# Routing of tokens to experts: GpSimd in place of VectorE makes the low halves of the token rows

## The chip, the cores and the metric

The kernel runs on one core of one Trainium2 chip. The metric is device time in microseconds. Three runs of the kernel before took 1812.97, 1812.97 and 1817.88 us, median 1812.97. Engines are called as in the profile: PE (TensorE), DVE (VectorE), ACT (ScalarE), POOL (GpSimd), SP (SyncE, which issues DMAs here).

## The reference

Four residual blocks follow each other on `x` of 4 x 1024 tokens with 256 features: cross-attention, a mixture of experts, cross-attention, a mixture of experts. The change lies in what comes ahead of both mixtures. Cut to that:

```python
x = x + _L0_xattn_ref(ctx_768, _layernorm(x), ...)
x = x + _L0_ffn_ref(_layernorm(x), router_w, w1, b1, w2, b2)   # 8 experts, 2 per token
x = x + _L1_xattn_ref(_layernorm(x), ctx_768, ...)
x = x + _L1_ffn_ref(_layernorm(x), gate_w, w1, w2, w3)         # 8 experts, 2 per token

# in both mixtures, z = layernorm(x):
logits = z @ router                # (tokens, 8)
probs = softmax(logits)
top_w, top_idx = top_k(probs, 2)
top_w = top_w / (sum(top_w) + 1e-9)
out = sum over the two chosen experts of top_w * expert(z)
```

## The kernel before

The 4096 tokens are 32 tiles of 128 rows (`T` = 32, `TB` = 8 tiles to a batch, `B` = 4 batches). They stay in SBUF in `g.x` (`x_sb` in the profile). The kernel is a chain of stages, each with one instruction stream per engine: attention, `route`, `experts`, attention, `route`, `experts`. `route` (line 816 on) is run once for each layer; the profile names its tiles with the prefix `e_`.

`route` normalises each tile to `z`, a ring of `R` = 4 buffers in f32, and does two things with it. PE transposes it (L898), ACT copies the transpose out (L938) and PE multiplies it with the router for the logits (L907). And the row is stored for the experts as two f16 halves, high and low, which together hold the f32 value: ACT writes the high half as a cast of `z` (L943, `token_high`), and DVE writes the low half as `z` minus the high half (L989, `token_low`). Both halves take the place of the tile of `x` in SBUF (`parts` is `g.x` seen as f16). SP stores a batch of them to memory once its 8 low halves are done, and then issues two loads of expert weights (`bring_home`).

DVE's stream sets the order of this first part. It centers tiles 0 to 3 (`center`, L984). Then it goes through t = 0 to 31: the low half of tile t, which waits for the high half of t; then `center(t + 4)`, which waits until the low half of t is done, since it takes over the same buffer of the ring. Some tiles have more behind them. At t = 1 stand the statistics of the last batch (`summarise`, L312 to L322), for which POOL makes the reciprocal roots (L328). At t = 2 DVE waits until POOL has made its constants (`p_step`, L882 to L889). At t = 10, 18 and 26 `choose` runs for the batch before: it copies the logits of 8 tiles (L1004) and finds the two best experts in a chain of small steps, each of which waits for the one ahead (L1006 to L1021). At t = 13, 21 and 29 `weigh` makes the shares. The fourth `choose` comes behind the loop.

ACT goes through the tiles with a copy and a high half each. At t = 12, 20 and 28 it makes the exponentials of the batch before (L949, L950), for which it waits for the last step of `choose`.

In the second part of `route` DVE, ACT and PE turn the choices into lists of slots for the experts (L1054 to L1108). They need all four choices. The first indirect DMA of `experts` (L1197) gathers token rows by these lists.

POOL in `route` had only the roots, one memset, one affine select and six iotas.

Of the kernel before, what the change touches and what calls it, by code (L numbers as in the profile page):

```python
# [21 lines left out]
ALU = mybir.AluOpType  # L22
# [3 lines left out]
P = 128  # L26
B = 4
S = 1024
T = B * S // P
TB = S // P  # L30
D = 256
# [12 lines left out]
E = 8  # L44
# [259 lines left out]
def summarise(dve, g, run, t0, t1, twice):  # L304

    seen = 7 * (run - 1)
    tmp, ve = g.stat_tmp[:, :, t0:t1], g.stat_ve[:, t0:t1]
    stats, steps = g.stats[:, t0:t1, :], g.stat_steps  # L310

    dve.tensor_tensor(tmp[:, 0, :], stats[:, :, 1], stats[:, :, 4], ALU.add).then_inc(steps, 1)  # L312
    dve.tensor_tensor(tmp[:, 1, :], stats[:, :, 1], stats[:, :, 4], ALU.subtract).then_inc(steps, 1)
    dve.tensor_tensor(tmp[:, 2, :], stats[:, :, 2], stats[:, :, 5], ALU.add).then_inc(steps, 1)
    dve.wait_ge(steps, seen + 3)
    dve.tensor_scalar(g.mean[:, t0:t1], tmp[:, 0, :], 0.5, None, ALU.mult).then_inc(steps, 1)
    dve.tensor_tensor(tmp[:, 3, :], tmp[:, 1, :], tmp[:, 1, :], ALU.mult).then_inc(steps, 1)
    dve.wait_ge(steps, seen + 5)
    dve.scalar_tensor_tensor(tmp[:, 0, :], tmp[:, 3, :], D / 4, tmp[:, 2, :], ALU.mult, ALU.add).then_inc(steps, 1)
    dve.wait_ge(steps, seen + 6)  # L320
    grow, eps = (1.0 + LN_EPS, LN_EPS ** 2) if twice else (1.0, LN_EPS)
    dve.tensor_scalar(ve, tmp[:, 0, :], grow / D, eps, ALU.mult, ALU.add).then_inc(steps, 1)  # L322


def roots(pool, g, run, t0, t1):

    pool.wait_ge(g.stat_steps, 7 * run)
    pool.tensor_tensor(g.rstd[:, t0:t1], g.stat_ve[:, t0:t1], g.neghalf[:, t0:t1], ALU.pow).then_inc(g.stat_roots, 1)  # L328
# [455 lines left out]
C = 2  # L784
NT = (2 * B * S + E * (C * P - 1)) // (C * P)
# [7 lines left out]
LAST = (B - 1) * TB  # L793
# [13 lines left out]
def route(nc, g, layer):  # L807
# [7 lines left out]
    R = 4  # L815
# [3 lines left out]
    with ExitStack() as st:  # L819
        m = Mem(nc, st)  # L820
        nm = g.name
        z = m.sb(nm("z"), [P, R, D])
        parts = g.x[:].bitcast(F16)
# [5 lines left out]
        upper = m.sb(nm("upper"), [P, P])  # L829
        rev = m.sb(nm("rev"), [P, E])  # L830
        tiles = m.sb(nm("tiles"), [P, NT, E])
        ecol = m.sb(nm("ecol"), [P, NT])
        lanes = m.sb(nm("lanes"), [P, P])
        blocks = m.sb(nm("blocks"), [P, NT * C])
        spare = m.sb(nm("spare"), [P, NT * C])
        ids = m.sb(nm("ids"), [P, 2, T])
# [6 lines left out]
        cnt, cumt, base = (m.sb(nm(f"e{i}"), [P, E]) for i in range(3))  # L843
        passed = m.sb(nm("passed"), [P, T + 1, E])
# [8 lines left out]
        z_done, hi_done, lo_done = m.sem(nm("z_")), m.sem(nm("hi")), m.sem(nm("lo"))  # L853
        chosen, shifted, lanes_known = (m.sem(nm(n)) for n in ("chosen", "shifted", "lanes_known"))
        scanned = m.sem(nm("scanned"))
        t_done, ev, lg_done, p_step = m.sem(nm("t")), m.sem(nm("ev")), m.sem(nm("lg")), m.sem(nm("p"))
# [7 lines left out]
        @block.sync  # L864
        def _(sp):
            def store(b):
                sp.wait_ge(lo_done, TB * (b + 1))
                sp.dma_start(g.zrows[b * S:(b + 1) * S, :].rearrange("(t p) d -> p t d", p=P),
                             parts[:, b * TB:(b + 1) * TB, :]).then_inc(stored, 16)

            bring_home(sp, g, layer, 0)
            for b in range(B):
                store(b)
                if 1 + b < AHEAD:
                    bring_home(sp, g, layer, 1 + b)
            sp.wait_ge(stored, 16 * B)
            sp.wait_ge(g.x_home, 16 * B * (layer + 1))

        @block.gpsimd
        def _(pool):  # L880
            roots(pool, g, 3 + 2 * layer, LAST, T)
            pool.memset(passed[:, 0, :], 0.0).then_inc(p_step, 1)  # L882
            pool.affine_select(out=upper[:], in_=g.ones[:], compare_op=ALU.is_gt, fill=0.0, base=0,
                               pattern=[[1, P]], channel_multiplier=-1).then_inc(p_step, 1)
            for out, pattern, start, by_row in (
                    (rev[:], [[-1, E]], E, 0), (tiles[:], [[1, NT], [0, E]], 0, 0), (lanes[:], [[1, P]], 0, 0),
                    (blocks[:], [[P, NT * C]], 0, 0), (spare[:], [[0, NT], [P, C]], B * S, 1),
                    (ids[:], [[0, 2], [P, T]], -B * S, 1)):
                pool.iota(out, pattern=pattern, base=start, channel_multiplier=by_row,  # L889
                          allow_small_or_imprecise_dtypes=True).then_inc(p_step, 1)  # L890
        @block.tensor
        def _(pe):
            def turn(t):
# [86 lines left out]
        def _(dve):  # L980
            def center(t):
                if t >= R:
                    dve.wait_ge(t_done, t - R + 1)
                dve.tensor_scalar(z[:, t % R, :], g.x[:, t, :], g.mean[:, t:t + 1], g.rstd[:, t:t + 1],  # L984
                                  ALU.subtract, ALU.mult).then_inc(z_done, 1)

            def token_low(t):
                dve.wait_ge(hi_done, t + 1)
                dve.tensor_tensor(parts[:, t, D:2 * D], z[:, t % R, :], parts[:, t, 0:D], ALU.subtract  # L989
                                  ).then_inc(lo_done, 1)  # L990

            n = [0]

            def step(ins):
# [5 lines left out]
            def choose(b):  # L1000

                ts = slice(b * TB, (b + 1) * TB)
                dve.wait_ge(lg_done, (b + 1) * TB)
                step(dve.tensor_copy(lg[:, ts, :].rearrange("p t e -> p (t e)"), plg[b % 2][:, 0:TB * E]))  # L1004
                for src, top, oh in ((lg, m0, oh0), (l2, m1, oh1)):
                    step(dve.tensor_reduce(top[:, ts], src[:, ts, :], AX.X, ALU.max))  # L1006
                    step(dve.tensor_tensor(wk[:, ts, :], src[:, ts, :], over_e(top[:, ts], TB), ALU.is_equal))
                    step(dve.tensor_tensor(wk2[:, ts, :], wk[:, ts, :], over_t(rev[:], TB), ALU.mult))
                    step(dve.tensor_reduce(r0[:, ts], wk2[:, ts, :], AX.X, ALU.max))
                    step(dve.tensor_tensor(oh[:, ts, :], over_t(rev[:], TB), over_e(r0[:, ts], TB), ALU.is_equal))  # L1010
                    if src is lg:
                        step(dve.scalar_tensor_tensor(l2[:, ts, :], oh0[:, ts, :], MASKED, lg[:, ts, :],
                                                      ALU.mult, ALU.add))
                dve.tensor_tensor(wk[:, ts, :], oh0[:, ts, :], oh1[:, ts, :], ALU.add).then_inc(chosen, 1)
                if b == B - 1:
                    dve.wait_ge(chosen, B)
                    for e in range(E):
                        dve.tensor_tensor_scan(passed[:, 1:T + 1, e], g.ones[:, 0:T], wk[:, :, e], 0.0,
                                               ALU.mult, ALU.add).then_inc(scanned, 1)
                step(dve.tensor_tensor(l2[:, ts, :], lg[:, ts, :], over_e(m0[:, ts], TB), ALU.subtract))  # L1020
                dve.tensor_tensor(sm[:, ts], m1[:, ts], m0[:, ts], ALU.subtract).then_inc(shifted, 1)  # L1021

            def weigh(b):

                ts = slice(b * TB, (b + 1) * TB)
                dve.wait_ge(ex_done, 2 * b + 2)
                step(dve.tensor_reduce(den[:, ts], ex[:, ts, :], AX.X, ALU.add))
                step(dve.tensor_scalar(den[:, ts], den[:, ts], 1e-9, 1.0, ALU.mult, ALU.add))
                step(dve.tensor_tensor(den[:, ts], den[:, ts], e1[:, ts], ALU.add))
                step(dve.reciprocal(share[:, 0, ts], den[:, ts]))  # L1030
                step(dve.tensor_tensor(share[:, 1, ts], share[:, 0, ts], e1[:, ts], ALU.mult))
# [2 lines left out]
            for t in range(R):  # L1034
                center(t)
            for t in range(T):
                token_low(t)
                if t + R < T:
                    dve.wait_ge(lo_done, t + 1)
                    if t + R == LAST:  # L1040
                        dve.wait_ge(g.stat_roots, 3 + 2 * layer)
                    center(t + R)
                if t == 1:
                    summarise(dve, g, 3 + 2 * layer, LAST, T, False)
                if t == 2:
                    dve.wait_ge(p_step, 8)
                if t >= TB and t % TB == AFTER:
                    choose(t // TB - 1)
                if t >= TB and t % TB == AFTER + 3:
                    weigh(t // TB - 1)  # L1050
# [846 lines left out]
```

## Time and profile before

| | |
|---|---|
| median of three runs | 1812.97 us |
| the profiled execution | 1812.47 us |
| its span | 1810.7 us |
| DVE busy | 1110.4 us (61%) |
| POOL busy | 706.7 us (39%) |
| low halves (L989) | 64 on DVE, 415 to 426 ns each, 536.5 to 1402.3 us |
| routing of layer 0 | 534.9 to 621.3 us |
| routing of layer 1 | 1358.9 to 1444.9 us |

The span is the time from the first to the last instruction of the profiled execution, 1.8 us less than the execution's own time. A row in order of time gives start and duration in microseconds, the engine, the line, the operation, what is written and read, and in brackets how long the engine had been idle and what ended that. "DVE L984" is `center`, "DVE L989" the low half, "ACT L943" the high half. In the rows `x_sb` stands for the two halves too, since they lie in its place.

### The profile page before, as it was taken

What the parts mean: (1) busy time and instruction counts of PE and PEld (TensorE: products, weight loads), DVE (VectorE), ACT (ScalarE), POOL (GpSimd) and SP (SyncE); (2) the same over time, 40 slices, a digit from 0 to 9 for tenths busy, and PEclk for the clock granted to TensorE, in tenths of its full rate; (3) what the DMA queues carried; (4) which work ended last, traced back from release to release, by engine and by line L of the source; (5) the groups of instructions that cost most, each with busy time, mean ns of one, the idle gap of its engine ahead of it and who ended that gap; (6) DMA issues with size and microseconds to landing.
All of it is one profiled execution on the core that took longest, in us unless ns stands there. A gap on an engine that the chain in (4) does not pass through costs nothing. (4 is left out here: it accounts for less than half of the span.)

```text
span 1810.7 us, 39194 instructions
## 1 busy us (share of the span) xinstructions
PE 1554.4 (86%) x12604; PEld 1143.3 (63%) x12605; DVE 1110.4 (61%) x1945; ACT 824.6 (46%) x1516; POOL 706.7 (39%) x521
## 2 busy tenths in 40 slices
PE   4798798897977599999999994899978599999996
PEld 1433334234337478888888881777768478888885
DVE  4687787787868634444554441888868744444443
ACT  1563654645633355555554440566754322222221
POOL 2401303104000125555554431677760045556554
PEclk9899899898985799999999995799995799999998
DMA  4321311322228245555542222200006243333333
GB/s 134 111 71 47 123 62 46 116 69 97 67 89 279 90 148 139 139 139 139 136 116 46 45 34 52 70 25 24 25 1 233 86 134 61 58 58 59 60 59 44
DMA packets 104311, 159.85 MB, mean 88 GB/s; under 512 B 10810, under 2 KB 69998, under 8 KB 104110
## 3 DMA queue, kind: packets, MB, share of 16 engines
q1 hardware_dynamic: 73007, 117.52, 19.9%
q0 software_dynamic: 29952, 40.91, 12.9%
q8 instruction: 43, 0.70, 0.2%
q10 hardware_dynamic: 1279, 0.46, 0.1%
q14 instruction: 30, 0.25, 0.0%
HBM read 91.49 MB, written 67.37 MB: 88 GB/s over the span
## 5 line engine op out<-in xcount | busy, mean ns | idle before, releaser
L1243 PE MATMUL e_ph<-e_zTt,weights_a 128*128 128x256 f16 x3744 | 426.7, 275 | 29.9 <-issue 27.5
L1243 PEld LDWEIGHTS e_ph<-e_zTt,weights_a 128*128 x3744 | 361.6, 98 | 94.6 <-issue 50.4
L1376 DVE TENSOR_TENSOR e_hl<-e_h,e_hh 128x512 f16<-128x512 f32 x156 | 104.5, 690 | 230.7 <-ACT e_hh L1342 230.7
L1197 POOL DMA_INDIRECT e_zt<-token_parts,slot_token x156 | 163.4, 1048 | 210.6 <-issue 198.8
L1328 ACT ACTIVATE e_h<-e_ph,e_b 128x256 f32<-128x256 f32 x312 | 130.6, 470 | 234.9 <-PE e_ph L1243 157.5
L1207 POOL DMA_INDIRECT token_rows<-e_ysb,slot_token x78 | 148.2, 1900 | 208.9 <-DVE e_ysb L1393 194.7
L1257 PE MATMUL e_pyt<-weights_b,e_hh 128*128 x1248 | 210.7, 273 | 0.7 <-DVE e_ysb L1393 0.7
L640 ACT ACTIVATE probs<-lower_banks,shift 128x1024 f32<-128x1024 f32 x128 | 137.5, 1110 | 92.1 <-PE lower_banks L500 91.7
L1207 POOL DMA_INDIRECT out_dram<-e_ysb,slot_token x78 | 124.4, 1595 | 131.0 <-DVE e_ysb L1397 107.4
L1257 PE MATMUL e_pyt<-weights_b,e_hl 128*128 x624 | 170.1, 273 | 0.0
L1367 DVE SCALAR_TENSOR_TENSOR e_g<-e_ph,e_h 128x512 f32<-128x512 f32 x78 | 53.9, 691 | 173.8 <-PE e_ph L1243 173.8
L660 DVE TENSOR_TENSOR acc<-acc,probs 128x1024 f32<-128x1024 f32 (+1 forms) x112 | 136.8, 1222 | 21.4 <-ACT probs L640 18.2
L513 PE MATMUL middle_banks<-probs,v 128*64 128x512 f32 (+1 forms) x576 | 142.9, 607 | 1.0 <-ACT probs L640 1.0
L1257 PEld LDWEIGHTS e_pyt<-weights_b,e_hh 128*128 128x128 f16 x1248 | 122.1, 98 | 14.7 <-issue 1.0
L1331 ACT ACTIVATE e_h<-e_ph 128x512 f32<-128x512 f32 x78 | 46.6, 597 | 170.5 <-PE e_ph L1243 170.5
L500 PE MATMUL lower_banks<-qT,kT 64*128 64x512 f16 (+1 forms) x864 | 114.5, 397 | 2.9 <-ACT kT L607 2.9
L1257 PE MATMUL e_pyt<-weights,e_hh 128*128 x624 | 108.6, 273 | 0.3 <-DVE e_ysb L1397 0.3
L676 POOL COPY cshift<-shift 77x1 f32 x4 | 0.7, 183 | 255.7 <-PE middle_banks L474 255.7
L500 PEld LDWEIGHTS lower_banks<-qT,kT 64*128 64x128 f16 (+1 forms) x864 | 37.4, 99 | 99.9 <-ACT probs L640 41.9
L1709 POOL TENSOR_TENSOR s<-s,rs 128x1232 f32<-128x1232 f32 x32 | 72.7, 2272 | 51.7 <-DVE rs L1777 51.5
L1342 ACT CAST e_hh<-e_h 128x512 f16<-128x512 f32 x156 | 92.3, 619 | 0.0
L1612 PE MATMUL pt<-ident,s 128*77 128x128 f32 x512 | 73.8, 290 | 14.6 <-ACT pT L1675 7.0
(228 smaller groups left out, 2847.0 us busy)
## 6 DMA issues: line engine op xcount, KB each, us to landing
weight_parts<-w_split SPq DMA_DIRECT2D x32, 512.0 KB, 3.3
weights_a<-weight_parts SPq DMA_DIRECT2D x16, 1024.0 KB, 7.5
x_sb<-in_u SPq DMA_DIRECT2D x24, 512.0 KB, 5.1
weight_parts<-x_sb SPq DMA_DIRECT2D x24, 512.0 KB, 3.4
w_raw<-in_w1T SPq DMA_DIRECT2D x16, 512.0 KB, 4.4
w_raw<-in_w2T SPq DMA_DIRECT2D x16, 512.0 KB, 4.7
weights_b<-weight_parts SPq DMA_DIRECT2D x8, 1024.0 KB, 9.5
token_parts<-x_sb SPq DMA_DIRECT2D x8, 1024.0 KB, 5.3
```

What stands on the lines that cost most here:

```text
L500: last = pe.matmul(sc[0:rows(k), n % 2, j, :], kT[dims, kp, pair, k * P:k * P + rows(k)], qT[dims, qp, pair, half * HALF:(half + 1) * HALF ...
L513: last = pe.matmul(po[u % 2][j * HD0:(j + 1) * HD0, :], v[0:rows(k), k, h * HD0:(h + 1) * HD0], pr[0:rows(k), n % 4, j, :], start=(k == 0) ...
L640: act.activation(pr[0:r, n % 4], sc[0:r, n % 2], ACT.Exp, bias=bias).then_inc(e_done, 1)
L660: dve.tensor_tensor(acc[0:r, u % 2], acc[0:r, u % 2], pr[0:r, n % 4], ALU.add).then_inc(acc_done, 1)
L1197: pool.indirect_dma_start(zt[:, i % 2, c, :], None, g.zrows, at).then_inc(ld[i % 2], 16)
L1207: pool.indirect_dma_start(g.rows[layer], at, ysb[:, s, c, :], None, compute_op=ALU.add).then_inc(sto[s], 16)
L1243: last = pe.matmul(ph[:, q, f, :], up_w(wp, e, k, 2 * q + f), zTs[:, s, 2 * zp + k, :], start=(n == 0), stop=(n == 5))
L1257: last = pe.matmul(py[c][:, 0, :], hp[:, s, f, c * P:(c + 1) * P], down_w(wp, e, f), start=(n == 0), stop=(n == 3 * NF - 1))
L1328: last = act.activation(h32[:, q % 2, f, :], ph[:, q, f, :], ACT.Relu, bias=b1[:, bass.ds(e, 1), 2 * q + f], scale=1.0 / WS)
L1342: act.copy(hh[:, s, 2 * q:2 * q + 2, :], src[:, q % 2]).then_inc(hi_done, 1)
L1376: dve.tensor_tensor(hl[:, s, 2 * q:2 * q + 2, :], src[:, q % 2], hh[:, s, 2 * q:2 * q + 2, :], ALU.subtract).then_inc(lo_done, 1)
L1612: last = pe.transpose(pt[:, n % 2, h % 4, :], s[:, d % SLOT, h, :], g.ident[:])
```

## The change

`token_low` is taken out of DVE's stream and put into POOL's, with the same operands and semaphores. DVE's loop keeps its wait for the low half before each `center(t + 4)`; that low half now comes from another engine. POOL makes the low halves of tiles 0, 1 and 2, then the roots and the constants as before, then the low halves of tiles 3 to 31.

```diff
         @block.gpsimd
         def _(pool):
-            roots(pool, g, 3 + 2 * layer, LAST, T)
-            pool.memset(passed[:, 0, :], 0.0).then_inc(p_step, 1)
-            pool.affine_select(out=upper[:], in_=g.ones[:], compare_op=ALU.is_gt, fill=0.0, base=0,
-                               pattern=[[1, P]], channel_multiplier=-1).then_inc(p_step, 1)
-            for out, pattern, start, by_row in (
...
+            def token_low(t):
+                pool.wait_ge(hi_done, t + 1)
+                pool.tensor_tensor(parts[:, t, D:2 * D], z[:, t % R, :], parts[:, t, 0:D], ALU.subtract
+                                  ).then_inc(lo_done, 1)
+
+            for t in range(T):
+                token_low(t)
+                if t == 2:
+                    roots(pool, g, 3 + 2 * layer, LAST, T)
+                    pool.memset(passed[:, 0, :], 0.0).then_inc(p_step, 1)
+                    pool.affine_select(out=upper[:], in_=g.ones[:], compare_op=ALU.is_gt, fill=0.0, base=0,
+                                       pattern=[[1, P]], channel_multiplier=-1).then_inc(p_step, 1)
+                    for out, pattern, start, by_row in (
...
@@ DVE @@
-            def token_low(t):
-                dve.wait_ge(hi_done, t + 1)
-                dve.tensor_tensor(parts[:, t, D:2 * D], z[:, t % R, :], parts[:, t, 0:D], ALU.subtract
-                                  ).then_inc(lo_done, 1)
-
...
             for t in range(T):
-                token_low(t)
                 if t + R < T:
                     dve.wait_ge(lo_done, t + 1)
                     if t + R == LAST:
```

## Rows read from the trace of the kernel before

**Rows 1.** The head of the page.
```profile
span 1810.7 us, 39194 instructions
```

**Rows 2.** Stretches, one round per layer: us, PE, PEld, DVE, ACT, POOL busy, clock, DMA share, GB/s.
```profile
549.40:560.30 10.90, 9.71 (x49) 9.31 (x50) 9.99 (x36) 5.51 (x18) 0.00 (x0) 0.50 0.79 277
...
1384.50:1395.50 11.00, 9.82 (x50) 9.42 (x49) 10.09 (x37) 5.62 (x19) 0.00 (x0) 0.50 0.71 240
```

**Rows 3.** Order of time, layer 0: its start, and the experts' first gather.
```profile
536.51 0.43 DVE L989 TENSOR_TENSOR x_sb<-e_z,x_sb 128x256 f16<-128x256 f32 x1 [0.27 <-ACT x_sb L943]
...
536.64 0.42 ACT L943 CAST x_sb<-e_z 128x256 f16<-128x256 f32 x1
...
536.98 0.41 DVE L984 TENSOR_SCALAR e_z<-x_sb,mean,rstd 128x256 f32<-128x256 f32 x1
...
537.76 0.41 DVE L984 TENSOR_SCALAR e_z<-x_sb,mean,rstd 128x256 f32<-128x256 f32 x1
...
539.17 1.74 POOL L328 TENSOR_TENSOR rstd<-stat_ve,neghalf 128x8 f32<-128x8 f32 x1 [82.79 <-DVE stat_ve L322]
...
543.01 0.42 DVE L989 TENSOR_TENSOR x_sb<-e_z,x_sb 128x256 f16<-128x256 f32 x1 [3.14 <-POOL e_ids L889]
...
543.94 0.69 PE L898 MATMUL e_pz<-ident,e_z 128*128 128x128 f32 x2 [2.18 <-DVE e_z L984]
...
621.27 1.21 POOL L1197 DMA_INDIRECT e_zt<-token_parts,slot_token x1 [78.30 <-issue]
```

**Rows 4.** Order of time, layer 0: the first choice and what follows it.
```profile
548.45 0.41 ACT L943 CAST x_sb<-e_z 128x256 f16<-128x256 f32 x1
...
548.89 0.43 DVE L989 TENSOR_TENSOR x_sb<-e_z,x_sb 128x256 f16<-128x256 f32 x1 [0.30 <-ACT x_sb L943]
...
549.35 0.41 DVE L984 TENSOR_SCALAR e_z<-x_sb,mean,rstd 128x256 f32<-128x256 f32 x1
...
549.62 0.41 ACT L943 CAST x_sb<-e_z 128x256 f16<-128x256 f32 x1
549.68 0.22 DVE L1004 COPY e_r<-e_plg 128x64 f32<-128x64 f32 x1
...
550.19 0.22 DVE L1007 TENSOR_TENSOR e_lane_hot<-e_r,e_c 128x64 f32<-128x64 f32 x1
...
550.80 0.41 ACT L943 CAST x_sb<-e_z 128x256 f16<-128x256 f32 x1
550.96 0.22 DVE L1010 TENSOR_TENSOR e_r<-e_rev,e_c 128x64 f32<-128x64 f32 x1
...
553.16 0.17 DVE L1021 TENSOR_TENSOR e_c<-e_c 128x8 f32<-128x8 f32 x1
...
553.36 0.26 ACT L949 ACTIVATE e_ex<-e_r 128x64 f32<-128x64 f32 x1 [2.16 <-DVE e_c L1021]
...
559.84 0.43 DVE L989 TENSOR_TENSOR x_sb<-e_z,x_sb 128x256 f16<-128x256 f32 x1
...
560.63 0.21 DVE L1004 COPY e_r<-e_plg 128x64 f32<-128x64 f32 x1
```

**Rows 5.** POOL's tensor_tensor of 128x256 in the first attention: ns min/median/max, starts.
```profile
L671 POOL TENSOR_TENSOR x_sb<-x_sb,bo_row x32: 722/732/1115, 54.5 to 443.5; 128x256 f32 x32
```

**Rows 6.** Order of time, first attention: DVE and POOL instructions that meet.
```profile
310.68 0.96 DVE L690 TENSOR_SCALAR z<-x_sb,mean,rstd 128x256 f32 x1
310.75 0.74 POOL L671 TENSOR_TENSOR x_sb<-x_sb,bo_row 128x256 f32 x1
...
319.34 0.68 DVE L717 TENSOR_TENSOR hl<-qk,hl 128x512 f16<-128x512 f32 x1
...
319.50 1.11 POOL L671 TENSOR_TENSOR x_sb<-x_sb,bo_row 128x256 f32 x1
...
430.90 0.75 POOL L671 TENSOR_TENSOR x_sb<-x_sb,bo_row 128x256 f32 x1
430.98 1.22 DVE L717 TENSOR_TENSOR hl<-qk,hl 128x512 f16<-128x512 f32 x1
```

More of the change, by code:

```diff
@@ L880, in _ @@
         def _(pool):
-            roots(pool, g, 3 + 2 * layer, LAST, T)
-            pool.memset(passed[:, 0, :], 0.0).then_inc(p_step, 1)
-            pool.affine_select(out=upper[:], in_=g.ones[:], compare_op=ALU.is_gt, fill=0.0, base=0,
-                               pattern=[[1, P]], channel_multiplier=-1).then_inc(p_step, 1)
-            for out, pattern, start, by_row in (
[L886 to L890, printed above, removed]
+            def token_low(t):
[10 more added lines that the diff above has]
+                    for out, pattern, start, by_row in (
+                            (rev[:], [[-1, E]], E, 0), (tiles[:], [[1, NT], [0, E]], 0, 0), (lanes[:], [[1, P]], 0, 0),
+                            (blocks[:], [[P, NT * C]], 0, 0), (spare[:], [[0, NT], [P, C]], B * S, 1),
+                            (ids[:], [[0, 2], [P, T]], -B * S, 1)):
+                        pool.iota(out, pattern=pattern, base=start, channel_multiplier=by_row,
+                                  allow_small_or_imprecise_dtypes=True).then_inc(p_step, 1)
         @block.tensor
```

## The prediction
> **What bounds the kernel now.** I read the page's head first (the span, [rows 1]), then the routing stages by stretches, then their order in time, because the change touches nothing outside the two routing stages: in layer 0 from 535 us to the first gather of the experts at 621.27 [rows 3], in layer 1 from about 1359 to 1445 us. Each has a part with 32 token tiles (about 44 us) and a part that works on the chosen slots. Only the first part contains the moved instruction, and everything in the second waits for its last choice, so a microsecond in the first part is a microsecond of the whole.
>
> The stretches say at first sight that VectorE is the limit: in a round of eight tiles it is busy 9.99 of 10.90 us in layer 0 and 10.09 of 11.00 in layer 1 [rows 2]. The order in time says otherwise. In the round of the first choice [rows 4] the high half of tile 10 is written by ACT at 548.45 for 0.41 us. VectorE's low half of that tile starts at 548.89, and had sat idle 0.30 us for ACT. Then come center(14) at 549.35, the choice's first read at 549.68, and a chain of dependent small steps to its last at 553.16. ACT waits 2.16 us for that last step before its exponentials (553.36), and it has no copy for TensorE in that time. Then ACT and TensorE work down the next tiles until the high half of tile 18 releases the low half at 559.84, and the next choice starts at 560.63. So a round is a closed loop: high, low, center, choice, exponentials, five more tiles, high. It takes 560.63 - 549.68 = 10.95 us. VectorE's other seven low halves of a round lie in the shade of the tile pitch of 549.62 - 548.45 = 1.17 us, which TensorE and ACT set between them [rows 4]. Only one low half in eight is on the loop.
>
> **The change part by part.** It removes 64 VectorE instructions of 0.42 us, 26.9 us of its work, and adds 64 to POOL. Off the loop they give nothing back: after a choice, center(15) starts 0.42 us earlier, but TensorE is then held by ACT's copies, not by a missing z.
>
> The price of a low half on POOL is not in the trace. The nearest row is POOL's tensor_tensor of the same 128x256 size, all f32: minimum 722, median 732, maximum 1115 ns [rows 5]. Bounds: 0.43 us if POOL were as fast as VectorE [rows 4], 1.11 us by the maximum. I take 0.73, because size and number of operands agree; what is open is the f16 operand and output.
>
> *The loop, directly.* Low goes from 0.43 to 0.73 us and one hop between engines is added, about 0.03 us (low ends at 549.32, center starts at 549.35 [rows 4]; I take one hop more of that size). That is +0.33 us a round, and nothing is behind it to take it up. Three rounds in each layer contain it: tiles 10, 18 and 26. The fourth choice starts when the last logits are there, and no low half stands before it.
>
> *The loop, by collision.* POOL will now compute while VectorE does, and the trace shows what that costs [rows 6]. At 310.68 VectorE's tensor_scalar with mean and rstd, the same form as center, took 0.96 us instead of 0.41 beside POOL's tensor_tensor of 310.75 to 311.49; it ended 0.15 us after POOL. At 430.98 a VectorE tensor_tensor with two SBUF inputs took 1.22 instead of 0.68 beside POOL's of 430.90 to 431.65. The other way round, VectorE's from 319.34 made POOL's at 319.50 take 1.11. Whoever is second waits for nearly all of the first. The Trainium skill's page "SBUF — State Buffer" (section "SBUF: two separate sides") says the same as a rule: the port pair shared by VectorE and GpSimd is an exclusive lock, held for the whole instruction, and a VectorE instruction takes it with two SBUF inputs or in a 2-port mode. The three rows agree. By a rule of shared bandwidth instead, the collisions would cost little and the sum would be the first rival's.
>
> Placed in time: the high half of tile 10 ends at 548.86, POOL's low runs to about 549.65, center(14) from 549.68, and the choice starts some 0.33 us later, at 550.01. Now POOL's low of tile 11 runs from its high's end, 550.03 [rows 4], for 0.73 us, to about 550.80. The choice's first two-input step (L1007, 0.51 us after its start in [rows 4], so 550.52 now, for 0.22) ends at about 550.89 instead of 550.74: +0.15. POOL's low of tile 12 follows its high's end at 551.21 and runs to about 552.0; the second of the choice's later two-input steps (L1010, by then at about 551.44) has to wait to about 552.08 instead of ending at 551.66: +0.42. Tile 13's high waits for the exponentials, so no third one falls in. Together +0.57 us a round; bounds 0 (no collision) and 1.46 (both lows in full). The loop term is 0.33 + 0.57 = 0.90 a round, 2.7 us for three.
>
> *The start.* VectorE waits here for POOL's constants, through the second half's statistics [rows 3]. The first low now runs on POOL from about 536.57 to 537.30. The second is ready at once (its high half ends at 537.06) and starts without a gap, just when center(4) is released, so center(4) waits for it: end 538.13 instead of 537.39. The third low (POOL, to 538.70, held 0.15 us by center(4)) does the same to center(5): 538.85 instead of 538.17. The statistics follow it, and POOL's root starts at about 539.85 instead of 539.17: +0.68. The constants then end at 543.66. The low of tile 3 waits behind them on POOL (544.34), and the low of tile 4, ready long before, follows without a gap and holds center(7) again, to 545.17 instead of 543.88. TensorE waits for exactly this z: its transpose at 543.94 [rows 3] moves by +1.3 us. Bounds: +0.5 with no collision (0.3 + 0.2 for the longer lows and their hops), +2.1 if each blocked low costs 1.11. What was late before goes on being late, only later; from here the tile pitch of 1.17 us hides POOL (0.73) and the centers.
>
> *SP.* The stores of token rows wait for the same count as before and leave up to 1 us after their tile. The weight loads queued behind them on SP move with them. The slot part, from the last choice at about 579 to 621.27 [rows 3], covers them. No DMA is added, and POOL has no other work in this part than the roots and constants, queued behind three lows that are over before their input is there.
>
> **Sum.** Per layer 1.3 + 2.7 = 4.0 us, twice 8.0 us. The profiled execution took 1812.47 us (span 1810.7 [rows 1] and 1.8 around it), so 1820.5; the median of the runs is 0.5 above that execution, so **1821 us**, +0.44%.
>
> **The rivals.**
> *Collisions don't reach the path.* If POOL's reads and VectorE's small steps of 64 elements slip past each other, what is left is 0.5 at the start and 3 x 0.33: 1.5 us a layer, 3.0 in all, 1816. For it: the colliding rows are of 256 and 512 elements, none as short as the choice's. Against it: the lock falls to whoever starts first, and POOL's 0.73 us are long whatever VectorE brings.
>
> *VectorE is the bound after all.* Then with 8 x 0.42 us less a round it falls to TensorE's floor, 8 x 1.17 = 9.36 instead of 10.95, so -1.6 us in each of three rounds, -4.8 a layer, -9.5 in all: 1803.5. For it: 9.99 us busy of 10.90 [rows 2]. Against it: VectorE's 0.30 us wait for ACT at the loop's low and ACT's 2.16 us wait for the choice [rows 4]. It decides if center, not the high half, is what a round waits for; that I don't find.
>
> *The mixed low is dearer on POOL.* At 1.11 us (the maximum of [rows 5]) the loop term grows by 0.38, the two blocking lows by 0.38 each, and the start by 0.38 for each of four lows: 1.5 + 3 x 1.1 = 4.9 us a layer, so 8.0 + 9.8 = 17.8: 1831. Above 1.17 us POOL itself would set the pitch of all 32 tiles, and each 0.1 us would add 6 us more. For it: nothing in the trace has an f16 operand in a POOL tensor_tensor. The Trainium skill's "GPSIMD Engine Reference" (section "Performance versus the Vector engine") counts about 2.6 cycles of 1.2 GHz an element for two inputs, an estimate of 0.56 us for 256 before the fixed part, and speaks against moving elementwise work to it; with the fixed part that would be near the 0.73 of the row, so by it the forecast's sum stands.
>
> **How the numbers follow.** The forecast has 0.50, collisions off the path 0.20, the dearer low 0.15, VectorE as the bound 0.07; the remaining 0.08 are mixtures, 0.05 of them near no change and 0.03 slower. A difference under 0.3% (5.4 us) is no change for this kernel, so below 1807.5 is faster and above 1818.4 slower. Faster 0.07, same 0.20 + 0.05 = 0.25, slower 0.50 + 0.15 + 0.03 = 0.68. The forecast's own range is 1818.5 to 1825; the range for 8 in 10 takes in the first rival's 1816 and the lower part of the dear low: 1815 to 1829.
>
> **What would show it.** Right: POOL rows of 128x256 with an f16 output near 0.73 us; center(7) ending about 1.3 us later relative to the first center than now; the distance from one choice's first step to the next 0.9 us longer, 11.85; in the choice a two-input step of over 0.5 us; ACT's wait for the choice longer than 2.16 us; the slot part unchanged in length. Wrong: rounds shorter than 10.95 us (VectorE was the bound), rounds of 11.3 us with all steps of the choice at 0.22 us (no collision on the path), POOL rows of over 1 us, or a change in a stretch outside the two routing stages, which I have no reason for.

## The result: 0.36% slower, 1822.36 us after 1816.62

Seven runs of each kernel, taken together, gave a median of 1822.36 us (1821.25 to 1823.42) for the changed kernel and 1816.62 us (1812.97 to 1818.18) for the kernel before. The ratio is 1.0036 with a 95% interval of [1.0025, 1.0048], that is 4.5 to 8.7 us. The profiled execution of the changed kernel took 1821.83 us, its span is 1820.1.

Within the two profiled executions the difference can be placed. I call "token part" the time from the first center of a layer to the first step of its fourth choice, "start" its piece up to the first choice, "round" the distance from one choice to the next (two of them), and "last" the distance from the third choice to the fourth. All are differences of starts in the order of time:

| us | start | rounds | last | token part | slot part, to the first gather |
|---|---|---|---|---|---|
| before, layer 0 | 14.82 | 10.95, 10.93 | 7.42 | 44.12 | 42.29 |
| before, layer 1 | 14.84 | 10.94, 10.94 | 7.43 | 44.15 | 41.83 |
| after, layer 0 | 16.18 | 11.79, 11.79 | 8.05 | 47.81 | 42.16 |
| after, layer 1 | 16.14 | 11.78, 11.80 | 8.06 | 47.78 | 41.66 |

The token parts are 3.69 and 3.63 us longer, 7.3 together. The spans differ by 9.4; of the other 2.1 us, 1.4 stand ahead of the first routing (first center at 536.29 instead of 534.86), where nothing was changed. I count that as a difference between two executions and not as the change's. What is left, 7.3 of 1813 us or 0.40%, lies in the measured interval.

The first round in order of time, DVE and POOL, with the highs of ACT. "DVE L993" is now the center, "POOL L883" the low half, "ACT L952" the high half, L1008 to L1025 the choice. The counterpart is [rows 4].
```profile
550.96 0.41 ACT L952 CAST x_sb<-e_z 128x256 f16<-128x256 f32 x1
...
551.44 0.67 POOL L883 TENSOR_TENSOR x_sb<-e_z,x_sb 128x256 f16<-128x256 f32 x1 [0.51 <-ACT x_sb L952]
552.13 0.41 ACT L952 CAST x_sb<-e_z 128x256 f16<-128x256 f32 x1
552.14 0.42 DVE L993 TENSOR_SCALAR e_z<-x_sb,mean,rstd 128x256 f32<-128x256 f32 x1 [0.76 <-POOL x_sb L883]
552.47 0.22 DVE L1008 COPY e_r<-e_plg 128x64 f32<-128x64 f32 x1
552.61 0.67 POOL L883 TENSOR_TENSOR x_sb<-e_z,x_sb 128x256 f16<-128x256 f32 x1 [0.51 <-ACT x_sb L952]
552.73 0.22 DVE L1010 TENSOR_REDUCE e_c<-e_r 128x8 f32<-128x64 f32 x1
552.98 0.38 DVE L1011 TENSOR_TENSOR e_lane_hot<-e_r,e_c 128x64 f32<-128x64 f32 x1
...
553.79 0.67 POOL L883 TENSOR_TENSOR x_sb<-e_z,x_sb 128x256 f16<-128x256 f32 x1 [0.51 <-ACT x_sb L952]
553.91 0.62 DVE L1014 TENSOR_TENSOR e_r<-e_rev,e_c 128x64 f32<-128x64 f32 x1
...
556.51 0.17 DVE L1025 TENSOR_TENSOR e_c<-e_c 128x8 f32<-128x8 f32 x1
...
556.71 0.26 ACT L958 ACTIVATE e_ex<-e_r 128x64 f32<-128x64 f32 x1 [3.00 <-DVE e_c L1025]
...
564.26 0.22 DVE L1008 COPY e_r<-e_plg 128x64 f32<-128x64 f32 x1
```
DVE now sits idle 0.76 us for POOL before the center that leads to the choice, and the low stands between a high and that center with 0.67 us. The choice has two long steps, 0.38 and 0.62 us; all others are at 0.17 to 0.23, as before. The first overlaps POOL's low of 552.61 to 553.28 and ends 0.08 us after it, the second POOL's of 553.79 to 554.46 and ends 0.07 after it. ACT waits 3.00 us for the choice instead of 2.16.

One round of each layer by stretches (columns as in [rows 2]):
```profile
550.90:562.60 11.70, 9.67 (x49) 9.27 (x49) 8.15 (x28) 5.48 (x19) 5.36 (x9) 0.50 0.77 268
1378.70:1390.50 11.80, 9.77 (x49) 9.37 (x50) 8.16 (x29) 5.58 (x19) 5.45 (x8) 0.50 0.67 225
```
VectorE's busy time in a round fell from about 10 to 8.15 us, and the round became longer. Over the whole span it fell by 14.9 us (1110.4 to 1095.5) where 26.9 us of work went away: the time in which a step is blocked counts as busy.

The start of layer 0, and below it the waits of the token part, longest in total first; the counterpart is [rows 3].
```profile
536.29 1.38 DVE L993 TENSOR_SCALAR e_z<-x_sb,mean,rstd 128x256 f32<-128x256 f32 x4 [0.54 <-PEq L339]
...
537.99 2.02 POOL L883 TENSOR_TENSOR x_sb<-e_z,x_sb 128x256 f16<-128x256 f32 x3 [80.23 <-ACT x_sb L952]
...
538.70 1.46 DVE L993 TENSOR_SCALAR e_z<-x_sb,mean,rstd 128x256 f32<-128x256 f32 x2 [1.02 <-POOL x_sb L883]
...
541.16 1.74 POOL L328 TENSOR_TENSOR rstd<-stat_ve,neghalf 128x8 f32<-128x8 f32 x1 [1.16 <-DVE stat_ve L322]
...
546.44 0.69 PE L907 MATMUL e_pz<-ident,e_z 128*128 128x128 f32 x2 [3.26 <-DVE e_z L993]
```
```profile
POOL x_sb L883 <- ACT x_sb L952: 99.7, 23, 80.2
ACT e_zTs L947 <- PE e_pz L907: 33.3, 23, 18.4
DVE e_z L993 <- POOL x_sb L883: 14.2, 14, 4.3
ACT e_ex L958 <- DVE e_c L1025: 9.0, 3, 3.0
```
Two centers (tiles 4 and 5) take 1.46 us where alone they take 0.41 each. POOL waits 1.16 us for the statistics before its root, so the roots and constants are late because the statistics are, and not because three lows stand ahead of them. The root starts 4.87 us after the first center instead of 4.31, TensorE's transpose of tile 7 10.15 instead of 9.08: +0.56 and +1.07.

POOL's low halves as a group (ns min/median/max, starts):
```profile
L883 POOL TENSOR_TENSOR x_sb<-e_z,x_sb x64: 667/667/815, 538.0 to 1410.9; 128x256 f16<-128x256 f32 x64
```

### The profile page after: what moved, and what is told of

The parts are those of the page before. It is cut to its first block and busy times, and to the rows that moved or that the text cites. A ratio compares the mean times of both kernels' runs of the same rounds, so it can differ in the third digit from the quotient of the medians.

```text
span 1820.1 us, 39188 instructions
## 1 busy us (share of the span) xinstructions
PE 1553.6 (85%) x12604; PEld 1142.5 (63%) x12605; DVE 1095.5 (60%) x1881; ACT 827.0 (45%) x1516; POOL 750.0 (41%) x585
## 5 line engine op out<-in xcount | busy, mean ns | idle before, releaser
L883 POOL TENSOR_TENSOR x_sb<-e_z,x_sb 128x256 f16<-128x256 f32 x64 | 43.0, 680 | 129.6 <-ACT x_sb L952 129.5
```

## The experiments

Each kernel was compared with runs of the kernel before on the same chip. e5 and e6 were run once each, so only their distances are used. `OWN` is the set of tiles whose low half DVE makes itself, where the kernel before had it; POOL makes the others. In both streams a low waits for the one before it when another engine makes that.

```diff
+                if t not in OWN:          # POOL
                     token_low(t)
...
             for t in range(T):            # DVE
+                if t in OWN:
+                    token_low(t)
                 if t + R < T:
                     dve.wait_ge(lo_done, t + 1)
```

| | ratio to before [95%] | start | rounds | last | token part |
|---|---|---|---|---|---|
| the change | 1.0036 [1.0025, 1.0048] | 16.18, 16.14 | 11.79 | 8.05 | 47.81, 47.78 |
| e1_no_meet | 1.0025 [1.0013, 1.0036] | 16.34, 16.14 | 11.23 | 7.50 | 46.30, 46.11 |
| e2_own_low | 1.0041 [1.0027, 1.0056] | 15.89, 15.88 | 11.79 | 8.34 | 47.80, 47.80 |
| e3_start | 1.0031 [1.0020, 1.0041] | 15.37, 15.14 | 11.78 | 8.05 | 46.99, 46.77 |
| e4_all_three | 1.0006 [0.9996, 1.0015] | 15.08, 15.09 | 10.98 | 7.50 | 44.55, 44.56 |
| e5_late_pool | one run, 1816.57 us | 16.17, 16.26 | 11.42 | 7.69 | 46.71, 46.80 |
| e6_late_dve | one run, 1813.83 us | 15.07, 14.83 | 10.92 | 7.35 | 44.25, 44.02 |
| e7_open_pool | 0.9991 [0.9981, 1.0000] | 15.10, 15.11 | 10.93, 10.80 | 6.68 | 43.51, 43.54 |
| e8_open_dve | 0.9975 [0.9966, 0.9985] | 12.48, 13.76 | 10.91 | 7.17 | 41.47, 42.76 |
| e9_constants | 0.9972 [0.9955, 0.9989] | 12.46, 13.83 | 10.95 | 7.43 | 41.78, 43.14 |

### No low half beside a choice: e1_no_meet

`OWN = {t for t in range(TB, T) if t % TB in (3, 4)}`

> VectorE makes the low halves of tiles 11, 12, 19, 20, 27 and 28 itself, right behind the choice, as in the kernel before; POOL makes the other 26 of a layer. So no POOL instruction runs beside a choice. Lock theory: the two long steps of each choice (0.38 and 0.62 us) fall to 0.22, the rounds from 11.79 to about 11.23 us, the last distance (third choice to fourth) from 8.06 to about 7.5, the token part of a layer from 47.8 to about 46.1, the whole 3.4 us less than the changed kernel, 1819. The start (first center to first choice) stays at 16.2. Rival, what the round lost is the longer low half and its hops alone and the long steps are a mark of the profile that costs nothing: rounds stay at 11.79, 1822.

Measured: rounds 11.23 and last 7.50, what was expected. The two steps that were long, in the second round:
```profile
565.28 0.23 DVE L1022 TENSOR_TENSOR e_lane_hot<-e_r,e_c 128x64 f32<-128x64 f32 x1
...
566.06 0.22 DVE L1025 TENSOR_TENSOR e_r<-e_rev,e_c 128x64 f32<-128x64 f32 x1
```
So the long steps are what they seem: POOL's low halves of tiles 11 and 12 cost the loop 0.56 us a round, and the rival falls. The start is as in the changed kernel in layer 1 (16.14) and 0.16 us above it in layer 0.

### Only the low half on the loop back to VectorE: e2_own_low

`OWN = {t for t in range(TB, T) if t % TB == 2}`

> VectorE makes only the low halves of tiles 10, 18 and 26 itself, the three that stand on the loop; POOL makes the other 29 of a layer. The choice then starts 0.29 us earlier behind its high half, but POOL's lows of tiles 11 and 12 stay where they are. Lock theory: L1007's counterpart now meets the whole rest of the low of tile 11 (0.43 instead of 0.16 us more) and the later step that of tile 12 (0.43), so the choice gets longer by what it gained, and rounds stay within 0.1 of 11.79; whole kernel within 1 us of the changed one. Rival, the two terms simply add: rounds 11.50, token part 47.8 - 0.9 = 46.9, the whole 1.7 us less.

Measured: the token part is 47.80 in both layers, the rounds 11.79. Nothing is gained, and the trace shows where it went. The third choice of layer 1:
```profile
1390.23 0.67 POOL L886 TENSOR_TENSOR x_sb<-e_z,x_sb 128x256 f16<-128x256 f32 x1 [1.68 <-ACT x_sb L956]
1390.31 0.67 DVE L1022 TENSOR_TENSOR e_lane_hot<-e_r,e_c 128x64 f32<-128x64 f32 x1
...
1391.40 0.67 POOL L886 TENSOR_TENSOR x_sb<-e_z,x_sb 128x256 f16<-128x256 f32 x1 [0.51 <-ACT x_sb L956]
1391.53 0.62 DVE L1025 TENSOR_TENSOR e_r<-e_rev,e_c 128x64 f32<-128x64 f32 x1
```
The choice starts 0.29 us earlier against POOL's lows, and its first two-input step now lies wholly under the low of tile 11: 0.67 instead of 0.38 us. The 0.29 us that the start gains (15.89 instead of 16.18), the last distance gives back (8.34 instead of 8.05). The two terms of the loop do not add, because a blocked step ends with POOL's instruction wherever it began. When a blocked step ends is set by POOL's pace of one low per 1.17 us, not by the chain ahead of it.

### VectorE makes the first seven: e3_start

`OWN = set(range(7))`

> VectorE makes the low halves of tiles 0 to 6 itself, POOL those of 7 to 31. Lock theory of the start: the centers of tiles 4, 5 and 7 no longer wait for POOL's next low, the start (first center to first choice) falls from 16.2 to 15.1 us (before: 14.8, and 0.29 for the low of tile 10 on POOL), rounds stay at 11.79, the whole 2.1 us less than the changed kernel, 1820. Rival, the start is late because POOL's constants stand behind three lows: then they also move by less than 0.3 us here and the start stays above 15.8.

Measured: start 15.37 and 15.14, rounds unchanged. The token part is 0.82 and 1.01 us shorter than in the changed kernel; in layer 1 that is the expected 1.0. VectorE could go on behind the constants 8.17 us after the first center in layer 1 (1369.00 - 1360.83), against 8.15 before and 8.65 with the low halves on POOL (544.94 - 536.29). So 0.5 of the 1.07 us up to the transpose of tile 7 comes from the later constants, which the blocked centers 4 and 5 delayed, and the rest from the low of tile 3 and the blocked center(7) behind them. The rival is refuted in both of its parts: the constants moved by 0.48 us and not by less than 0.3, and the start fell below 15.8. The edit cannot part the two reasons by itself, since it also takes the three lows from ahead of the constants; that those did not delay them is read from POOL's wait of 1.16 us for the statistics, shown above.

In layer 0 everything up to the constants is 0.23 us later than in layer 1 (8.40 us, 544.63 - 536.23). Both layers run the same edit, so that is not its doing. It goes with the clock: TensorE's granted clock was already 0.64 in the stretch from 536 to 537, where it was 1.00 in the kernel before, and the first copy of a transpose came 1.19 us after the first center instead of 0.95.

### The three edits together: e4_all_three

`OWN = set(range(7)) | {t for t in range(TB, T) if t % TB in (2, 3, 4)}`

> The three edits together: VectorE makes the low halves of tiles 0 to 6 and of 10 to 12, 18 to 20 and 26 to 28, POOL the other 16 of a layer, so VectorE is still relieved of 6.7 us a layer. Theory (a round is a closed loop through one low half and the choice, VectorE's work beside it is free): start 14.8, rounds 10.95, token part 44.1, time as of the kernel before within 1 us. Rival (VectorE's busy time is worth something once POOL is out of the way of the loop): rounds below 10.8, token part below 43.5.

Measured: ratio 1.0006 [0.9996, 1.0015], rounds 10.98 and 7.50, start 15.1. One round of layer 1:
```profile
1377.20:1388.20 11.00, 9.81 (x50) 9.41 (x50) 9.15 (x33) 5.61 (x20) 3.65 (x5) 0.50 0.78 257
```
VectorE does 0.9 us less in it than in the kernel before, and the round is not shorter. Against e1 a round differs by the low of tile 10 alone, and is 0.25 us shorter, most of the 0.29 us that this low with its hops costs on POOL. The loss of the change is accounted for to 0.4 us a layer (44.55 against 44.12), of which the start holds 0.25. These 0.25 us are no cost of POOL's lows: they stand already at POOL's root, 4.57 us after the first center instead of 4.31, ahead of the first low on POOL. The granted clock was 0.60 and 0.62 in the first stretches here, and e6, with no low on POOL at all, has the same 0.24 us between its two layers (15.07 and 14.83), at 0.64 and 1.00.

### The exponentials later: e5_late_pool, e6_late_dve

```diff
-                if t >= TB and t % TB == AFTER + 2:     # ACT, exponentials
+                if t >= TB and t % TB == AFTER + 4:
...
-                if t >= TB and t % TB == AFTER + 3:     # DVE, weigh
+                if t >= TB and t % TB == AFTER + 5:
```
In the first the low halves are on POOL, in the second on VectorE.

> The changed kernel (all low halves on POOL) with ACT's exponentials two tiles later (behind tile 14 of a round instead of 12) and the shares two tiles later (15 instead of 13), so ACT no longer waits for the choice. The loop through the choice is then only that through the ring of four: low of tile 10, center(14), choice, center(15), TensorE's tile 15. Theory: TensorE has z up to tile 14 when the choice starts and runs dry before center(15): rounds about 10.7 us, 1.1 less than 11.79. Rival (TensorE's pitch alone sets the round once ACT is free): 9.4.

> The same two moves in the kernel before (low halves on VectorE). ACT's wait goes, and now VectorE is the limit: eight lows and centers (8 x 0.78), a choice of 3.6 and shares of 1.1 us make 10.9 to 11.0, so rounds stay at 10.9. Rival (ACT's wait was the only limit): rounds of 10.5 or less.

Measured, e5: rounds of 11.42, a miss by 0.7. ACT's stop had held back the highs of tiles 13 and 14. Without it their lows run beside the choice too: four of its steps now take 0.38, 0.63, 0.63 and 0.62 us, and the choice takes 5.0 us (1387.91 to 1392.92). TensorE then runs dry at tile 15, as foreseen, and ACT still waits a little:
```profile
1392.95 0.26 ACT L958 ACTIVATE e_ex<-e_r 128x64 f32<-128x64 f32 x1 [1.46 <-DVE e_c L1025]
...
1393.30 0.69 PE L907 MATMUL e_pz<-ident,e_z 128*128 128x128 f32 x2 [1.87 <-DVE e_z L993]
```
Measured, e6: rounds of 10.92, as expected. VectorE waits for no other engine in the round. The only waits are ACT's for TensorE and one of TensorE, 0.7 us, for a z. So in the kernel before, as far as one run and its trace show, two limits lie within 0.03 us of each other: the loop through the choice (10.95) and VectorE's own work with its gaps between steps (10.92). The change relieved the second and lengthened the first.

### The choice cut in two, constants first: e7_open_pool, e8_open_dve

Both have e5's edits, and:
```diff
-            roots(pool, g, 3 + 2 * layer, LAST, T)      # POOL: constants ahead of roots (and of all lows)
             pool.memset(passed[:, 0, :], 0.0).then_inc(p_step, 1)
...
+            roots(pool, g, 3 + 2 * layer, LAST, T)
...
-                if t >= TB and t % TB == AFTER:
-                    choose(t // TB - 1)
+                if t >= TB and t % TB in (AFTER, AFTER + 2):
+                    choose(t // TB - 1, (t % TB - AFTER) // 2)
```
The first half of `choose` finds the best expert, the second half the second best.

> The changed kernel with three more edits: exponentials and shares two tiles later, the choice cut into two halves (behind the centers of tiles 14 and 16), and POOL's constants ahead of its low halves. Theory: nothing on the loop waits long any more; VectorE needs 8 x 0.41 + 3.6 + 1.1 + collisions of up to 2 = about 10 us a round, TensorE 9.4, so rounds of 9.5 to 10; the start loses the wait for the constants and falls from 16.2 to about 13; the token part 40 to 41.5 us instead of 47.8, and the whole 12 to 15 us below the changed kernel, under the kernel before: 1806 to 1810. Rival (collisions eat what VectorE is relieved of): rounds of 10.9 as with the lows on VectorE.

> The same three edits in the kernel before, with the low halves on VectorE (constants ahead of the roots). Theory: VectorE is the limit, rounds 10.9 us; the start falls from 14.8 to about 12.5, the token part from 44.1 to about 42, the whole about 4 us below the kernel before. Rival (VectorE is not the limit here either): rounds of 9.4 to 10 as with POOL.

Measured, e7: rounds of 10.93 and 10.80, start 15.1; the hoped-for version does not come. The rival's number comes out, 10.9, and there are collisions. Over the second half of a choice in layer 1:
```profile
1390.11 1.09 DVE L993 TENSOR_SCALAR e_z<-x_sb,mean,rstd 128x256 f32<-128x256 f32 x2
1390.23 0.81 POOL L883 TENSOR_TENSOR x_sb<-e_z,x_sb 128x256 f16<-128x256 f32 x1 [0.51 <-ACT x_sb L952]
...
1391.62 0.57 DVE L1013 TENSOR_TENSOR e_lane_hot<-e_lane_hot,e_rev 128x64 f32<-128x64 f32 x1
...
1393.33 0.26 ACT L958 ACTIVATE e_ex<-e_r 128x64 f32<-128x64 f32 x1 [2.00 <-DVE e_c L1028]
```
ACT again waits 2.00 us, now for the second half, which stands two tiles later itself: moving both by two tiles had left the loop closed. The theory's "nothing waits long" was wrong for that reason. The rival's mechanism is not shown either: VectorE was busy for 8.54 of the 10.80 us of this round and not full. How much of the 10.9 is collision and how much the loop was not separated.

The start missed its 13 us, and the trace shows two things that go with it; their shares were not separated. TensorE's granted clock was 0.54 and 0.56 in the first stretches of the two layers, and the tiles had the slow pitch of 1.17 us from the third on. And with the constants first in its stream, POOL came to its first low 2.72 us after the first center instead of 1.70, and to its root at 5.86 instead of 4.87; the low of tile 3 stands behind the root, and VectorE sat idle for it before the next centers:
```profile
1370.18 2.36 DVE L993 TENSOR_SCALAR e_z<-x_sb,mean,rstd 128x256 f32<-128x256 f32 x4 [2.23 <-POOL x_sb L883]
```

Measured, e8: rounds of 10.91, as expected for VectorE as the limit. Its start is 12.48 us in layer 0, as expected, but 13.76 in layer 1. It is 0.25% faster than the kernel before.

### The constants alone: e9_constants

The kernel before with e8's first edit only (constants ahead of the roots).

> The kernel before, low halves on VectorE, with one edit: POOL's constants stand ahead of its roots. Theory (the gain of the two-halves run with VectorE's lows came from its start, not from the cut choice or the later exponentials): start 12.5 to 13.8 us instead of 14.8, rounds 10.95, last distance 7.4, token part 41.8 to 43.1, the whole 2.5 to 4 us under the kernel before. Rival (the cut choice carried the gain): start above 14.5, the whole within 1 us of the kernel before.

Measured: start 12.46 and 13.83, rounds and last as before, ratio 0.9972 [0.9955, 0.9989]. The token parts are 2.34 and 1.01 us shorter, 3.4 together. Up to 0.04 us a round and 0.26 in the last distance, what e8 gains in its distances is this one edit, and the two ratios can't be told apart. It takes away VectorE's wait of 3.14 us for constants [rows 3]. In layer 0 the last constant is done at 538.54, and the low half of tile 3, which had waited for it, starts without idle time:
```profile
540.85 0.42 DVE L989 TENSOR_TENSOR x_sb<-e_z,x_sb 128x256 f16<-128x256 f32 x1
```
The edit has nothing to do with who makes the low halves, and with them on VectorE it beats both kernels.

## Why the prediction was right

**The bound.** The step that decided the sign was to take a round as a closed loop through one low half in eight, against a VectorE busy for 9.99 of its 10.90 us. The runs bear it out: VectorE's busy time fell to 8.15 us and the round grew, and in e4 VectorE did 0.9 us less and the round was no shorter. ACT's 2.16 us wait for the choice belongs to that loop. But the other sign that the prediction names, VectorE's 0.30 us wait for ACT at the low, stands ahead of the first choice, before any round. At the low of tile 18, which closes the round, there is next to no wait in the kernel before:
```profile
559.40 0.41 ACT L943 CAST x_sb<-e_z 128x256 f16<-128x256 f32 x1
...
559.49 0.41 DVE L984 TENSOR_SCALAR e_z<-x_sb,mean,rstd 128x256 f32<-128x256 f32 x1
```
The high half ends at 559.81 and the low starts at 559.84 with no idle time in its row; the pairs of low and center ahead of it have a pitch of 0.78 us, and this one comes 0.80 after the last (559.04). VectorE was 0.02 us from being the limit itself, and the 10.92 us of e6 bear that out. The prediction did not see that tie. It did no harm, since the change took work from VectorE and made the loop longer. The rival "VectorE is the bound after all" (1803.5) was half right on where VectorE stood, and wrong on what relieving it gives.

**The price of a low half.** Taken as 0.73 us from POOL's 128x256 f32 row; measured median 0.667. With its f16 operand and output it was no dearer than the row in f32, so the rival of the dearer low falls. The low ran 0.07 us after its high where VectorE's had run 0.03 after, so low and hops together cost the round 0.29 instead of 0.33 us.

**The collisions.** Predicted +0.15 us for the first two-input step and +0.42 for a later one; measured +0.16 and +0.40. e1 takes them away and gets back 0.56 us a round. The first rival (collisions off the path, 1816) falls. The Trainium skill's "SBUF — State Buffer", section "Who interferes with whom", says that a VectorE instruction with at most one SBUF input, outside the 2-port modes, does not contend with GpSimd; the trace agrees: the reduce of 552.73 overlaps POOL's low of 552.61 and keeps its 0.22 us. One reading of [rows 6] was loose: "whoever is second waits" doesn't fit the first pair, where VectorE's row starts 0.07 us ahead of POOL's and VectorE waited all the same. Nothing in the sum hung on it.

**The round.** Predicted 11.85, measured 11.79. The last distance holds the collisions of the third choice and no low: predicted +0.57, measured +0.63.

**The start.** Predicted +1.3 us up to the transpose of tile 7, of it 0.68 up to the root. Measured +1.07 and +0.56. The mechanism is the one described (two centers in 1.46 us, center(7) behind the low of tile 4). Five lows stand on that way, each 0.06 us shorter than taken, which is most of the difference. The prediction also let center(4) hold the third low for 0.15 us; the first three lows took 2.02 us together, three times 0.67, so it was not held.

**The sum.** 8.0 us predicted, 7.3 in the token parts, 5.7 between the medians (1822.36 - 1816.62). The predicted 1821 rested on a median of 1813 for the kernel before; over more runs that kernel's median moved to 1816.6. That 1822.36 lies so near 1821 is therefore in part luck: the difference came out 2.3 us smaller than forecast and the level it starts from 3.65 us higher. What should be compared is the difference, and it is 0.7 to 2.3 us less than forecast.

**What was missed.** That the two loop terms don't simply add (e2), and that VectorE's own work stood 0.03 us behind the loop (e6). Neither changed this prediction; each would have misled a next one. The expectation for e5 forgot what the prediction itself says, that ACT's stop for the exponentials keeps the highs from tile 13 on, and so their lows, out of the choice.

## What to carry to other kernels

Ask of a busy engine which of its instructions stand on the loop that sets the pace: here one in eight of the moved ones did, and that one got slower. Before work is moved from VectorE to POOL, list what VectorE runs at the same time. In these traces a VectorE instruction with two SBUF inputs, or a tensor_scalar in f32, that started while a POOL tensor_tensor ran waited for its end, so a 0.22 us step became one of up to 0.67. A wait for constants that depend on nothing can be worth more than such a move: reordering POOL's own stream gave 0.28%, moving 27 us of VectorE's work to it cost 0.36%.

## What the hardware showed that was not expected

A blocked step of 64 elements ends 0.07 to 0.08 us after POOL's instruction, whatever was left of that when the step began. A small step is blocked as surely as a large one; in e2 it takes 0.67 us for 0.22 of work.

TensorE's clock fell from its higher level (2.4 GHz, granted 1.00) to its lower (1.2 GHz, 0.50) at different moments of the same work. In e8 the stretches of the two starts, 2.3 to 3.3 us and 1.5 to 2.5 us behind the first centers (534.66 and 1355.53):
```profile
537.00:538.00 1.00, 1.00 (x10) 0.92 (x10) 0.96 (x3) 1.00 (x4) 0.50 (x2) 0.90 1.03 230
...
1357.00:1358.00 1.00, 1.00 (x6) 1.00 (x7) 0.96 (x3) 0.72 (x3) 1.00 (x4) 0.50 1.05 313
```
In layer 0 the clock was at 0.50 only from the next stretch on. With it at 0.50 from 1357 on, the tiles of layer 1 followed each other at 1.17 us or more from the third on, those of layer 0 only from the sixth, and this goes with a start of 13.76 instead of 12.48 us. Collisions with POOL's constants are no rival: the first four centers take 1.77 us in both layers. In the kernel before the difference did not show (14.82 and 14.84), because the wait for constants lay over it. TensorE had sat idle for the first z for 2.52 us in layer 0 and 1.93 in layer 1; what decides the moment was not tried. A learner who compares starts of two kernels has to allow for it: the starts of the two layers of one run, which have the same code here, lie 0.2 us apart in e3 and e6 and 1.3 to 1.4 in e8 and e9.
